# Identity products on TensorE ahead of the first rows of four stages

## The chip, the core and the metric

The kernel runs on one core of one Trainium2 chip. The metric is the device time of one launch in microseconds (us). Engines are named as in the profile: PE is TensorE, DVE is VectorE, ACT is ScalarE, POOL is GpSimd, SP is SyncE, and PEld is the loading of weights into PE.

## What is computed

Four residual layers over `x` of 64 sequences of 64 rows of 256 numbers, cut here to their lines:

```python
x = x + tanh(g_xattn[0]) * _L0_xattn_ref(layernorm(x), ctx, ...)   # 8 heads, rotary, softmax
x = x + tanh(g_ffn[0])   * _L0_ffn_ref(layernorm(x), ...)          # 8 experts, best 2 of each row
x = x + tanh(g_xattn[1]) * _L1_xattn_ref(layernorm(x), ctx, ...)   # linear attention, relu features
x = x + tanh(g_ffn[1])   * _L1_ffn_ref(layernorm(x), ...)          # causal attention, then 16 experts, best 4
```

The first layer takes its tokens in blocks of channels: keys and queries are projected, turned by rotary tables, multiplied into scores, put through a softmax and multiplied with the values. In an expert layer each row goes through the experts that a small product (the router) chooses for it.

## The kernel before

The program is a row of stages, one after another, each a block in which every engine has its own list of instructions and waits on semaphores: softmax attention (lines 412 to 905), the first experts with the linear attention behind them (954 to 1483), causal attention (1935 to 2568), and the second experts (954 again). At the end of a block all engines meet before the next one starts. There is no scheduler: PE does its work in the order in which the code is written, and a wait in that order holds up everything behind it.

**Softmax attention** goes over 32 tiles of 128 rows, which the code calls `n`, in a loop over `i` from -5 to 34, and each step of the loop does a different part of several tiles. For tile `n`, `project(n, False)` (L846, L847) and `project(n, True)` (L846, L847 again) multiply the normalised rows and the context with the weights, in full fp32, at step `i = n - 4`; DVE multiplies the two results with the cosine and sine tables (L721), POOL adds them (L600), and DMAs lay the sum out into `soft_rep` (L504). Then `both(i, k)`, eight times in a step, makes score products: L816 (`soft_pa`) for a later tile, whose maxima DVE takes (L735), and L809 (`soft_pb`) for tile `i`, for ACT's exponential (L630). `values` (L830) multiplies with the values and L881 projects them. While `i` is negative there is no tile `i`: `both` then makes no `soft_pb`, and before the second half of `i = -2` it makes nothing at all. PE begins the loop when `soft_shift` (DVE, L710) is there.

**Each expert stage** starts with `b = -2` and `b = -1`. `turn_rows` (L1427) turns the 128 rows of a block, which a DMA brings as `moe_xs`, `up` (L1440) multiplies them with an expert's two input matrices, and `down` (L1459) with its output matrix.

**Causal attention** starts with constants; PE waits for `ca_hn`, turns the rows (L2549), and then `project` (L2396) makes the queries and keys of 128 columns at a time, five to a unit: `p` counts them. Each result is copied by ACT to `ca_q_f` (L2174), which has two buffers; SP's DMAs swap its halves (L2082), and DVE and POOL put the rotation together.

The matrix that all of these stages hold for turning rows is the identity in fp32: `soft_ident_f`, `ident` of the experts (a slice of `moe_held`), and `ca_ident`.

Of the kernel before, what the change touches and what calls it, by code (L numbers as in the profile page):

```python
# [20 lines left out]
PART = 128  # L21
# [24 lines left out]
def hold(eng, sem, count, held):  # L46

    if not (isinstance(count, int) and count <= 0):
        eng.wait_ge(sem, count)
        if not isinstance(count, int):  # L50
            eng.sem_inc(held, 1)

LOWEST, MARK = -3.0e38, -3.2e38
# [357 lines left out]
def stage_softmax_attention(nc, x_in, x_out, ctx, c):  # L412
# [8 lines left out]
    HEADS, GROUPS, KC, T, HALF, PAIRS = 16, 4, 8, 256, 2, 8  # L421
# [6 lines left out]
    with st:  # L428
# [77 lines left out]
        with nc.Block() as block:  # L506
# [278 lines left out]
            def _(pe):  # L785
# [5 lines left out]
                def both(i, k):  # L791

                    n, m = (i + 1, k + 4) if k < 4 else (i + 2, k - 4)
                    if live(i) and k == 0:
                        pe.wait_ge(peak_in[i % 2], 64 * (i // 2 + 1))
                    if live(n) and m == 0:
                        pe.wait_ge(rep_in[n % 4], REP * (n // 4 + 1))
                    for h in range(2):
                        if live(i):  # L800
                            past(pe, prob_ready, 2 * (PAIRS * i + k) + h - 1)
                        if live(n):
                            past(pe, a_done, 2 * (PAIRS * n + m) + h - 1)
                        for c in range(HALF):
                            out = slice((2 * h + c) * T, (2 * h + c + 1) * T)
                            if live(i):
                                g, rows = pair(k)
                                of, at = slice(32 * rows[h], 32 * rows[h] + SPLIT + 1), T + c * PART
                                mm = pe.matmul(p_b[:, out], rep[of, i % 4, g, at:at + PART], rep[of, i % 4, g, 0:T],  # L809
                                               start=True, stop=True)  # L810
                                if c == HALF - 1:
                                    mm.then_inc(b_ready, 1)
                            if live(n):
                                g, rows = pair(m ^ 1)
                                of, at = slice(32 * rows[h], 32 * rows[h] + SPLIT), c * PART
                                mm = pe.matmul(p_a[:, out], rep[of, n % 4, g, at:at + PART], rep[of, n % 4, g, T:2 * T],  # L816
                                               start=True, stop=True)
                                if c == HALF - 1:
                                    mm.then_inc(a_ready, 1)
# [15 lines left out]
                def project(n, rotated):  # L835
                    if not live(n):
                        return
                    r = int(rotated)
                    if rotated:
                        pe.wait_ge(cos_done, 2 * (n + 1))  # L840
                    else:
                        pe.wait_ge(xn_ready, n + 1)
                        pe.wait_ge(c_in_s[n // LOAD % 4], 16 * (n // RING + 1))
                        past(pe, sin_done, 2 * n)
                        past(pe, y_ready, n - 6)
                    pe.matmul(p_x[1][:, 0:T], w_in[:, r, :], xn[:, n % 2, :], start=True, stop=True)  # L846
                    pe.matmul(p_x[1][:, T:2 * T], w_in[:, 2 + r, :], ct[:, n % RING, :], start=True, stop=True  # L847
                              ).then_inc(qkrot_ready if rotated else qk_ready, 1)

                for i in every:  # L850
                    both(i, 0)
                    project(i + 4, False)
                    both(i, 1)
                    values(i - 1, 3)
# [99 lines left out]
def experts(nc, name, x_in, x_out, w_gate, w_up, w_down, c, EXPERTS, HIDDEN, TOP, norm, skip=None, then=None):  # L954
# [36 lines left out]
    with st:  # L991
# [75 lines left out]
        with nc.Block() as block:  # L1067
# [322 lines left out]
            def _(pe):  # L1390
# [72 lines left out]

                owner = {}
                for b in range(-2, ALL + 1):
                    if b + 2 < ALL:
                        turn_rows(b + 2)
                    if 0 <= b + 1 < ALL:
                        n = b + 1
                        if n == START[1]:  # L1470
                            pe.wait_ge(route.expert_ready, 1)
                        owner[n % 3] = pe.value_load(expert_of[0:1, n:n + 1],
                                                     min_val=0, max_val=EXPERTS - 1)
                        up(n, owner[n % 3])
                    if 0 <= b < ALL:
                        turn_act(b)
                    if b >= 1:
                        down(b - 1, owner[(b - 1) % 3])
                    routing(b)
# [455 lines left out]
def stage_causal_attention(nc, x_in, z_out, c):  # L1935
# [19 lines left out]
    with st:  # L1955
# [102 lines left out]
        with nc.Block() as block:  # L2058
# [330 lines left out]
            def _(pe):  # L2389
                pe.wait_ge(const_in, 16 * NCONST)  # L2390
                pe.wait_ge(const_r, 2)

                def products(out, pairs, start=True, stop=True):
                    todo = [xy for lh, ll, rh, rl in pairs for xy in ((lh, rh), (lh, rl), (ll, rh))]
# [4 lines left out]
                def project(u, m):  # L2399
# [5 lines left out]
                        pe.wait_ge(wlo_ready, ALL_Q)  # L2405
                    if m == 0 and kp == 0:
                        pe.wait_ge(htlo_ready, 2 * (ch + 1))
                    past(pe, qf_ready, p - 1 if p < EARLY else p)
                    if m == 0 and kp == 1:
                        past(pe, route.ht_ready, 2 * min(ch - 1, ROUTED))  # L2410
# [234 lines left out]
```

## Time and profile before

| what | value |
|---|---|
| median of 3 runs | 2581.12 us (2579.25 to 2589.17) |
| the profiled execution's own time | 2571.76 us |
| its span, first to last instruction | 2569.9 us |
| PE busy | 2199.1 us, 86% of the span |
| DVE busy | 1835.5 us, 71% |
| ACT, POOL busy | 1154.2 us, 1104.7 us |
| mean granted clock of TensorE | 0.926 |

The profile is of one execution. A row of the timeline shows a start, a duration, the engine, the line, what it writes and reads, how many instructions the row joins, and in brackets how long the engine stood idle ahead of it and for whom.
### The profile page before, as it was taken

How to read it: one execution, taken by the hardware profiler on the slowest of the kernel's cores; microseconds unless marked ns; L12 is line 12 of the kernel's file. 1: busy time of each engine (PE TensorE's matmuls, PEld its weight loads, DVE VectorE, ACT ScalarE, POOL GpSimd, SP SyncE). 2: the span in 40 equal slices, each digit the busy share in tenths (PEclk: the TensorE clock that was granted, in tenths of full speed). 3: DMA queues.
4: the chain of work that ended last, by engine and by line, in shares of the span. 5: the costliest groups of instructions: out<-in, count | busy, mean ns of one | idle time of the engine just before them, and what ended most of it. 6: DMA issues, size and time to landing. Idle time of an engine off the chain costs nothing. (4 is left out here: it accounts for less than half of the span.)

```text
span 2569.9 us, 60412 instructions
## 1 busy us (share of the span) xinstructions
PE 2199.1 (86%) x20880; PEld 1669.5 (65%) x20880; DVE 1835.5 (71%) x3965; ACT 1154.2 (45%) x2509; POOL 1104.7 (43%) x1111
## 2 busy tenths in 40 slices
PE   6889888886878799993899998999988699999990
PEld 4555555543766577762677777777766577888880
DVE  4888988872557787765878878878787374545754
ACT  2677767664534233323444444444333264333330
POOL 3454555565154500002555445455487600334736
PEclk9888989975899899997999999999999799999995
DMA  5455554442469523212332332322334382445854
GB/s 115 108 134 139 149 142 133 118 137 76 126 198 296 150 88 103 77 38 53 82 88 56 83 84 62 84 73 69 79 99 115 123 266 83 139 142 183 265 170 147
DMA packets 250435, 313.10 MB, mean 122 GB/s; under 512 B 45216, under 2 KB 202912, under 8 KB 250144
## 3 DMA queue, kind: packets, MB, share of 16 engines
q1 hardware_dynamic: 189168, 219.11, 30.7%
q0 software_dynamic: 26624, 58.79, 8.2%
q10 hardware_dynamic: 34352, 31.34, 3.6%
q8 instruction: 180, 2.95, 0.5%
q14 instruction: 111, 0.91, 0.1%
HBM read 122.40 MB, written 102.24 MB: 87 GB/s over the span
## 5 line engine op out<-in xcount | busy, mean ns | idle before, releaser
L2126 POOL TENSOR_TENSOR ca_qk<-ca_qk,ca_q_swap 128x512 f32<-128x512 f32 x160 | 248.9, 1556 | 366.6 <-DVE ca_q_swap L2304 366.1
L735 DVE TENSOR_REDUCE soft_top<-soft_pa 128x2 fp32r<-128x512 f32 x512 | 327.9, 683 | 83.0 <-PE soft_pa L816 80.2
L630 ACT ACTIVATE soft_prob<-soft_pb 128x512 f32<-128x512 f32 x512 | 286.1, 594 | 171.3 <-PE soft_pb L809 169.5
L809 PE MATMUL soft_pb<-soft_rep 32*128 32x256 f32 x1024 | 207.3, 359 | 53.2 <-DVE soft_top L735 27.6
L809 PEld LDWEIGHTS soft_pb<-soft_rep 32*128 32x128 f32 x1024 | 135.4, 211 | 170.3 <-issue 73.5
L816 PE MATMUL soft_pa<-soft_rep 31*128 31x256 f32 x1024 | 217.1, 366 | 5.9 <-DVE soft_top L735 3.5
L1459 PE MATMUL moe_py<-moe_w_d,moe_at 128*128 x788 | 212.7, 385 | 1.4 <-issue 0.8
L1440 PE MATMUL moe_pgu<-moe_w_hi,moe_xt_hi 128*128 x472 | 192.8, 408 | 22.7 <-DVE moe_xt_lo L1357 13.0
L2396 PE MATMUL ca_py<-ca_w_hi,ca_ot_hi 128*128 128x256 f32 x512 | 156.7, 306 | 38.3 <-DVE ca_ot_lo L2325 38.0
L1363 DVE TENSOR_TENSOR moe_act_f<-moe_silu,moe_pgu 128x256 f32<-128x256 f32 (+1 forms) x236 | 88.6, 375 | 131.5 <-ACT moe_silu L1258 131.2
L2304 DVE TENSOR_TENSOR ca_q_swap<-ca_q_swap,ca_sin_q 128x512 f32<-128x512 f32 x128 | 117.2, 916 | 82.0 <-DMA ca_q_swap<-ca_q_f 81.7
L1258 ACT ACTIVATE moe_silu<-moe_pgu 128x256 f32<-128x256 f32 (+1 forms) x236 | 82.4, 349 | 200.0 <-PE moe_pgu L1440 198.2
L1440 PE MATMUL moe_pgu<-moe_w_hi,moe_xt_lo 128*128 x472 | 171.1, 362 | 0.0
L1440 PE MATMUL moe_pgu<-moe_w_lo,moe_xt_hi 128*128 x472 | 170.7, 362 | 0.0
L830 PE MATMUL soft_po<-soft_prob,soft_vaug 128*32 128x256 f32 x2048 | 163.8, 446 | 0.0
L2188 ACT ACTIVATE ca_ot_hi<-ca_po 128x512 fp32r<-128x512 f32 x128 | 69.6, 595 | 209.7 <-PE ca_po L2494 209.7
L2396 PE MATMUL ca_pp<-ca_ht_hi,ca_w_hi 128*128 128x512 f32 x312 | 138.1, 443 | 22.8 <-ACT ca_q_f L2174 19.4
L1179 POOL DMA_INDIRECT moe_yg<-moe_ys_rows,moe_held x112 | 115.0, 1027 | 86.7 <-DVE moe_ys L1370 37.5
L1357 DVE TENSOR_TENSOR moe_xt_lo<-moe_pt,moe_xt_hi 128x256 fp32r<-128x256 f32 x236 | 99.5, 422 | 71.5 <-ACT moe_xt_hi L1253 70.2
L2396 PE MATMUL ca_py<-ca_w_lo,ca_ot_hi 128*128 128x256 f32 x512 | 150.3, 294 | 0.0
L2396 PE MATMUL ca_py<-ca_w_hi,ca_ot_lo 128*128 128x256 f32 x512 | 150.2, 293 | 0.0
L364 POOL DMA_INDIRECT moe_rows<-moe_x_new,moe_held x80 | 78.1, 976 | 163.3 <-DVE moe_ys L1370 91.5
(377 smaller groups left out, 6252.7 us busy)
## 6 DMA issues: line engine op xcount, KB each, us to landing
ca_q_swap<-ca_q_f SPq DMA_DIRECT2D x640, 64.0 KB
moe_xs<-moe_rows SPq DMA_DIRECT2D x236, 128.0 KB
soft_rep<-soft_parts SPq DMA_DIRECT2D x378, 64.0 KB
moe_rows<-soft_blank SPq DMA_DIRECT2D x27, 768.0 KB
moe_ys_rows<-moe_ys ACTq DMA_DIRECT2D x134, 128.0 KB, 1.7
moe_ys<-moe_ys ACTq DMA_DIRECT2D x102, 128.0 KB, 2.6
moe_xd<-scratch SPq DMA_DIRECT2D x64, 128.0 KB, 2.7
ca_vs<-ca_v SPq DMA_DIRECT2D x32, 256.0 KB, 3.8
```

The costliest lines, as they stand in the source:

```text
L630: act.activation(prob[:, k % 4, h, :], p_b[:, 2 * T * h:2 * T * (h + 1)], ACT.Exp).then_inc(prob_ready, 1)
L735: dve.tensor_reduce(heads[:, j, :, g], p_a[:, 2 * T * h:2 * T * (h + 1)].rearrange("p (c s) -> p c s", c=HALF), AX, ALU.max).then_inc(a_do ...
L809: mm = pe.matmul(p_b[:, out], rep[of, i % 4, g, at:at + PART], rep[of, i % 4, g, 0:T], start=True, stop=True)
L816: mm = pe.matmul(p_a[:, out], rep[of, n % 4, g, at:at + PART], rep[of, n % 4, g, T:2 * T], start=True, stop=True)
L830: mm = pe.matmul(p_o[g % 2][32 * j:32 * j + 32, 0:T], vaug[:, i % 4, sc, 4 * g + j, :], prob[:, (2 * g + j // 2) % 4, j % 2, sc * T:(sc + ...
L1179: pool.indirect_dma_start(out=yg[:, t % HELD, k, :], out_offset=None, in_=ys_rows[h], in_offset=bass.IndirectOffsetOnAxis(ap=slot_id[:, t, ...
L1357: dve.tensor_tensor(xt_lo[:, b % 2, :, :], p_t[b % 2][:, 0:DIM].rearrange("p (k t) -> p k t", k=KC), xt_hi[:, b % 2, :, :].bitcast(fp32), ...
L1440: mm = pe.matmul(p_gu[b % 2][:, 0:W2], x[:, b % 2, k, :], w, start=(n == 0), stop=(n == 3 * KC - 1))
L1459: mm = pe.matmul(p_y[b % 2][:, 0:DIM], at[:, b % 2, m, :], w_d[:, bass.ds(e, 1), m, :].rearrange("p a d -> p (a d)"), start=(m == 0), stop ...
L2126: pool.tensor_tensor(qk[:, u % 2, m, :], qk[:, u % 2, m, :], q_swap[:, p % 2, :], ALU.add).then_inc(qk_ready, 1)
L2304: dve.tensor_tensor(out.rearrange("p (b s) -> p b s", s=SEQ), src.rearrange("p (b s) -> p b s", s=SEQ), tab[int(m == RQ)][:].unsqueeze(1). ...
L2396: mm = pe.matmul(out, x, y, start=start and n == 0, stop=stop and n == len(todo) - 1)
```

## The change

A helper `warm` multiplies a 128x128 fp32 identity by itself a number of times, into a PSUM region that nobody reads before it is written again. PE's list gets it in five places; nothing else changes.

```diff
+def warm(pe, out, of, times):
+
+    for _ in range(times):
+        pe.matmul(out, of, of, start=True, stop=True)
...
@@ softmax attention, in both(i, k), for each h and c
                                 if c == HALF - 1:
                                     mm.then_inc(b_ready, 1)
+                            elif i < 0:
+                                warm(pe, p_o[0][:, T:T + PART], ident_f[:], 1)
...
                 for i in every:
                     both(i, 0)
+                    if i < -1:
+                        warm(pe, p_o[0][:, T:T + PART], ident_f[:], 8)
                     project(i + 4, False)
...
@@ both expert stages
                 for b in range(-2, ALL + 1):
+                    if b < 0:
+                        warm(pe, p_y[1][:, 0:PART], ident, 6 if b == -2 else 4)
                     if b + 2 < ALL:
                         turn_rows(b + 2)
...
@@ causal attention
                 pe.wait_ge(const_r, 2)
+                warm(pe, p_s[:, 0:PART], ident[:], 28)
...
                         pe.wait_ge(htlo_ready, 2 * (ch + 1))
+                    if 0 < p < M5 + 3:
+                        warm(pe, p_s[:, 0:PART], ident[:], 2)
                     past(pe, qf_ready, p - 1 if p < EARLY else p)
```

That is 192 products in softmax attention (32 in the eight calls of `both` of each of five steps, and 8 in each of four steps), 10 in each expert stage, and 42 in causal attention (28, and 2 ahead of each of seven projections).

PE's list at the start of softmax attention before; L846 and L847 are the projections, L881 the values' projection, L816 the first score products:

```order
2 L846 MATMUL soft_px<-soft_xn,soft_w_in 128x256
3 L847 MATMUL soft_px<-soft_ct,soft_w_in 128x256
4 L846 MATMUL soft_px<-soft_xn,soft_w_in 128x256
5 L847 MATMUL soft_px<-soft_ct,soft_w_in 128x256
6 L846 MATMUL soft_px<-soft_xn,soft_w_in 128x256
7 L847 MATMUL soft_px<-soft_ct,soft_w_in 128x256
8 L846 MATMUL soft_px<-soft_xn,soft_w_in 128x256
9 L847 MATMUL soft_px<-soft_ct,soft_w_in 128x256
10 L881 MATMUL soft_px<-soft_w_in,soft_ct 128x128 x2
```

The same stretch now, where L58 is the added product and all other lines have moved down (L855, L856 and L892 are the projections):

```order
2 L58 MATMUL soft_po<-soft_ident_f 128x128 x52
3 L855 MATMUL soft_px<-soft_xn,soft_w_in 128x256
4 L856 MATMUL soft_px<-soft_ct,soft_w_in 128x256
5 L58 MATMUL soft_po<-soft_ident_f 128x128 x8
6 L855 MATMUL soft_px<-soft_xn,soft_w_in 128x256
7 L856 MATMUL soft_px<-soft_ct,soft_w_in 128x256
8 L58 MATMUL soft_po<-soft_ident_f 128x128 x32
9 L855 MATMUL soft_px<-soft_xn,soft_w_in 128x256
10 L856 MATMUL soft_px<-soft_ct,soft_w_in 128x256
11 L58 MATMUL soft_po<-soft_ident_f 128x128 x8
12 L855 MATMUL soft_px<-soft_xn,soft_w_in 128x256
13 L856 MATMUL soft_px<-soft_ct,soft_w_in 128x256
```

Ahead of the first projection there now stand 52 products, ahead of the second 8, ahead of the third 32. A little later each score product of the steps -2 and -1 has one in front of it, the first four here (L825 is the score product, L816 before):

```order
22 L58 MATMUL soft_po<-soft_ident_f 128x128 x5
23 L825 MATMUL soft_pa<-soft_rep 128x256
24 L58 MATMUL soft_po<-soft_ident_f 128x128
25 L825 MATMUL soft_pa<-soft_rep 128x256
26 L58 MATMUL soft_po<-soft_ident_f 128x128
27 L825 MATMUL soft_pa<-soft_rep 128x256
28 L58 MATMUL soft_po<-soft_ident_f 128x128
29 L825 MATMUL soft_pa<-soft_rep 128x256
```

Before, these score products stood next to each other. At the start of causal attention PE now has this list, in which L2565 are the transposes (L2549 before) and L2410 the projections (L2396 before):

```order
4741 L58 MATMUL ca_ps<-ca_ident 128x128 x28
4742 L2565 MATMUL ca_p_t<-ca_ident,ca_hn 128x128 x4
4743 L2565 MATMUL ca_pp<-ca_ident,ca_hn 128x128 x4
4744 L2410 MATMUL ca_pp<-ca_ht_hi,ca_w_hi 128x512
4745 L2410 MATMUL ca_pp<-ca_ht_lo,ca_w_hi 128x512
4746 L2410 MATMUL ca_pp<-ca_ht_hi,ca_w_lo 128x512
4747 L2410 MATMUL ca_pp<-ca_ht_hi,ca_w_hi 128x512
4748 L2410 MATMUL ca_pp<-ca_ht_lo,ca_w_hi 128x512
4749 L2410 MATMUL ca_pp<-ca_ht_hi,ca_w_lo 128x512
4750 L58 MATMUL ca_ps<-ca_ident 128x128 x2
```

Before, the list of this block began with the transposes, and the second projection followed the first directly.

## Rows read from the trace of the kernel before

**Rows 1.** Stretches: us, busy time per engine (instructions), PEclk, DMA share, GB/s.

```profile
0.00:71.00 71.00, 45.64 (x165) 30.22 (x166) 34.48 (x78) 20.23 (x29) 21.19 (x28) 1.00 0.53 115
8.00:58.76 50.76, 33.70 (x94) 22.54 (x95) 25.71 (x60) 12.83 (x17) 12.85 (x13) 1.00 0.44 77
1163.00:1183.00 20.00, 0.00 (x0) 0.00 (x0) 12.94 (x34) 9.93 (x14) 4.62 (x7) 0.50 0.18 47
2064.00:2100.00 36.00, 35.89 (x185) 29.26 (x184) 31.99 (x65) 29.26 (x67) 0.00 (x0) 1.00 0.98 324
```

**Rows 2.** Timeline of PE, first rows of softmax: start, us, what, [idle before].

```profile
10.80 1.19 PE L846 MATMUL soft_px<-soft_xn,soft_w_in 128*128 128x256 f32 x2 [3.26 <-ACT soft_xn L655]
13.82 1.22 PE L846 MATMUL soft_px<-soft_xn,soft_w_in 128*128 128x256 f32 x2 [0.97 <-DVE soft_by_cos L721]
...
34.59 0.80 PE L816 MATMUL soft_pa<-soft_rep 31*128 31x256 f32 x4 [2.45 <-DMA soft_rep<-soft_parts]
...
38.04 1.39 PE L816 MATMUL soft_pa<-soft_rep 31*128 31x256 f32 x4 [0.49 <-DVE soft_top L735]
39.62 1.39 PE L816 MATMUL soft_pa<-soft_rep 31*128 31x256 f32 x4 [0.18 <-DVE soft_top L735]
...
58.76 0.55 PE L809 MATMUL soft_pb<-soft_rep 32*128 32x256 f32 x1 [0.28 <-DVE soft_top L735]
```

**Rows 3.** Timeline of DVE, the same stretch.

```profile
7.66 0.28 DVE L710 TENSOR_SCALAR soft_shift<-soft_px,soft_cols,soft_gate 128x1 f32<-128x1 f32 x1 [0.50 <-PE soft_px L787]
...
38.87 1.29 DVE L735 TENSOR_REDUCE soft_top<-soft_pa 128x2 fp32r<-128x512 f32 x2 [0.28 <-PE soft_pa L816]
```

**Rows 4.** Timeline of PEld and PE: fp32 passes of 128 columns or fewer.

```profile
35.31 0.93 PEld L881 LDWEIGHTS soft_px<-soft_w_in,soft_ct 128*128 128x128 f32 x4 [0.23 <-issue]
70.64 0.53 PEld L881 LDWEIGHTS soft_px<-soft_w_in,soft_ct 128*128 128x128 f32 x4
70.70 0.66 PE L881 MATMUL soft_px<-soft_w_in,soft_ct 128*128 128x128 f32 x4
458.68 3.43 PEld L252 LDWEIGHTS soft_px<-soft_r_picked,soft_r_ones 128*128 128x128 f32 x30
```

**Rows 5.** Timeline of PE: fp32 passes of 256 columns in the second experts.

```profile
2251.57 1.03 PE L1459 MATMUL moe_py<-moe_w_d,moe_at 128*128 x4
```

**Rows 6.** Timeline of PE: one product in each tile of softmax.

```profile
52.37 0.69 PE L877 MATMUL soft_px<-soft_ident,soft_top 128*128 128x128 f32 x2
70.36 0.50 PE L877 MATMUL soft_px<-soft_ident,soft_top 128*128 128x128 f32 x2
...
104.47 0.44 PE L877 MATMUL soft_px<-soft_ident,soft_top 128*128 128x128 f32 x2
119.75 0.44 PE L877 MATMUL soft_px<-soft_ident,soft_top 128*128 128x128 f32 x2
```

**Rows 7.** Timeline around the start of causal attention, PE and DVE.

```profile
1157.81 1.13 PE L1818 MATMUL la_py<-la_w_out,la_o_t 128*128 128x256 f32 x4 [0.47 <-ACT la_o_t L1715]
1170.03 0.19 DVE L2249 CAST ca_mask_r<-ca_mask 128x64 fp32r<-128x64 f32 x1
1183.53 1.09 PE L2549 MATMUL ca_p_t<-ca_ident,ca_hn 128*128 128x128 f32 x4 [24.59 <-ACT ca_hn L2203]
...
1186.98 0.76 PE L2396 MATMUL ca_pp<-ca_ht_hi,ca_w_hi 128*128 128x512 f32 x1 [1.50 <-DVE ca_ht_lo L2385]
...
1190.10 0.40 PE L2396 MATMUL ca_p_t<-ca_ht_lo,ca_w_hi 128*128 128x512 f32 x1
```

**Rows 8.** Timeline of PE, starts of the two expert stages.

```profile
644.90 0.69 PE L1427 MATMUL moe_pt<-moe_held,moe_xs 128*128 128x128 f32 x2 [8.97 <-DMA moe_xs<-moe_rows]
...
2056.22 0.69 PE L1427 MATMUL moe_pt<-moe_held,moe_xs 128*128 128x128 f32 x2 [14.95 <-DMA moe_xs<-moe_rows]
...
2058.16 0.79 PE L1440 MATMUL moe_pgu<-moe_w_hi,moe_xt_hi 128*128 x1 [0.17 <-issue]
...
2063.87 0.40 PE L1448 MATMUL moe_pat<-moe_held,moe_act_f 128*128 128x128 f32 x2
```

## The prediction

> **What bounds the kernel now.** I read the shares of the engines first: PE is the busiest, but at the places that the change touches it is idle for part of the time, so each place has to be read for itself. Then the stretches and the timeline of PE there.
>
> *First rows of softmax.* From 8 us, when DVE's `soft_shift` ends (7.66 + 0.28) [rows 3], to 58.76, when the first `soft_pb` is made [rows 2], PE is busy 33.7 of 50.8 us [rows 1]. Its waits are short ones, for the normalised rows, for the cosine product and for `soft_rep` [rows 2]: a chain that goes from engine to engine and back. The column of the granted clock shows 1.00 up to 71 us [rows 1], but nothing is recorded so early, and the passes say otherwise: four loads of one shape take 0.93 us at 35.31 and 0.53 us at 70.64 [rows 4]. So until about 70 us PE runs at its lower level, 1.2 GHz, and the idle 17 us would grow to about 34 if its 33.7 us of work ran at the other.
>
> *Later stages.* Causal attention starts with PE idle for 24.59 us; the clock stands at 0.50 through 1163 to 1183 [rows 1, 7], and passes shorten at 1190.1 [rows 7]. The first experts' PE waits 8.97 us for its first rows, the second experts' 14.95; in the latter passes shorten at 2063.87 [rows 8].
>
> **The price of one added product.** It is two passes of 128 columns in fp32. Thirty loads of passes of that kind take 3.43 us, 0.114 each [rows 4], so 0.23 us a product at 2.4 GHz. The bound above is a short group: two products take 0.66 us from first start to last end, 0.33 each [rows 4]. The bound below is 0.21: the thirty loads less the tail of the last one. At 1.2 GHz four loads take 0.93 us [rows 4]; less the tail of the last that is about 0.21 a pass, 0.43 a product. I take 0.23, since PE will have long rows of them, as in the thirty, and 0.43 while the clock is still low. How long that is: in causal attention 3.1 us pass from the first projection at 1186.98 to the short pass at 1190.10 [rows 7], in the second experts 5.7 us from 2058.16 to 2063.87 [rows 8]. I take 5.
>
> The Trainium skill ("TensorE: Matmul & The Clock Gate", Part 4) says that transposes against an identity do not raise the clock in the way that other products do. Here the added ones are ordinary products, and no run here shows what a row of identity products alone does; by that rule, if it held for them, the rival "the clock stays down" below would be the result.
>
> **Softmax, step by step** (PE's list; 192 products):
>
> 1. Ahead of the first projection stand 52 products, and PE can start them at 8.0. 5 us at the low clock pass some 11.6 of them, the other 40.4 take 9.3: the first projection starts at 22.3. It started at 10.80 [rows 2]. So 11.5 us late; PE had only 3.26 us to give away there.
> 2. From there to the first score product PE has six projections, 92 products (8, 32, 8, 32, 8 and 4) and the values' projection. A projection is four passes of 256 columns: 1.03 us [rows 5], and about 1.0 when the next one follows. 6.0 + 92 x 0.23 + 0.5 = 27.7, so the first score product would start at 50.0, before at 34.59 [rows 2]: 15.4 late. Does another chain end later? From the second projection at 13.82 to the score product were 20.8 us [rows 2], through DVE, POOL, ACT and the DMAs into `soft_rep`; the second projection now starts at 22.3 + 1.0 + 1.8 = 25.1, so `soft_rep` is there at about 45. PE is last.
> 3. From there to `soft_pb`: before, 24.2 us, twelve pairs of score products. A pair takes 1.58 us (38.04 to 39.62): 0.83 until DVE starts on it (38.87), 0.65 for DVE's half of 1.29, and 0.1 back [rows 2, 3]. With the products in it PE needs 4 x (0.23 + 0.12) = 1.4 a pair (four score passes take 0.80 at the low clock [rows 2], so about 0.12 each at the high one), and DVE can start about as late as before, since four passes have come in front and its own run twice as fast. I take 1.6, so 19.2; the other work in the stretch was 24.2 - 19.0 = 5.2 and becomes about 2.9. Together 22.1: `soft_pb` starts at 72.1, before at 58.76: **13.3 us late**.
> 4. Then the row itself gains: with the clock up from the start. From one `L877` to the next, the first tile took 17.99 us, the next two 34.11 together, and the one after 15.28 [rows 6]. I take 16.5 for the first: **1.5 less**, between none and 2.7.
>
> Nothing takes the delay back later: all 32 tiles follow one after another, and all stages after them.
>
> **Causal attention.** The 28 products may start once `ca_mask_r` is there, 1170.2 [rows 7]: 5 us low and 16.4 x 0.23 = 3.8, so they end near 1179, hidden in the idle time before 1183.53; at 0.43 each they would end at 1182.2, still hidden. What they buy: the transposes and the first projection, 6.6 us from 1183.53 to 1190.10 with 1.50 of waiting among it [rows 7], are PE's at the low clock for at most 4.6 us on the path, of which half could go. But then PE stands idle again for 4.5 us, and the last time it stood idle, from 1158.94, the clock was down by 1163 [rows 1, 7]. So it may be down again before the transposes. **0.7 less**, between 2.3 less and 1 more: the two products ahead of each later projection cost at most 0.46 to 0.86 us each where PE does not wait, and there the swaps by SP's DMAs are later anyway.
>
> **Experts.** Six products at the low clock are 2.6 us, against idle times of 8.97 and 14.95 us [rows 8], a part of which lies before the block opens, so up to 0.6 may stick out; the four ahead of the second transposes are 1.7 us, hidden in the first stage, and in the second they push the first `up` back by about 0.6. What they buy is an earlier rise: in the second stage at most half of the 5.7 us from 2058.16 to 2063.87, 2.9. But from 2064 to 2100 the DMA engines are at 0.98 [rows 1], so PE will meet the next rows' transfers instead. **0.7 less** in the first (2 less to 0.6 more), **0.5 less** in the second (2.4 less to 0.6 more).
>
> **The sum**: 13.3 - 1.5 - 0.7 - 0.7 - 0.5 = 9.9 us more. Against the profiled execution's own 2571.76 that is 2581.7; the median of the runs is 9.4 above that execution, and I put the same 9.9 on it: **2591.0 us**, 0.4% slower. Low end: 5 us of low clock less 0.9, 0.21 for a product 2.6 less, pairs by 0.1 less 1.2, and the four gains at their best, 5.9 more of them: about 0 in all, 2581. High end, with 0.26 a product and the gains at their worst: 9.9 + 0.3 + 4 + 1 + 4.7, some 20, 2601.
>
> **Rivals.**
>
> - *Each product costs what a lone one does*, 0.33. Then 132 products ahead of the score products cost 13 more, and a pair becomes PE's, 4 x (0.33 + 0.12) = 1.8, 2.4 more over twelve: 2606. For it: only loads and short groups are seen, no row of fp32 products of 128 columns. Against: the thirty [rows 4]. 15%.
> - *The clock stays down.* 52 x 0.43 puts the first projection at 30.4; the way to the score products is 12 + 92 x 0.43 + 1 = 53, a pair 4 x 0.63 = 2.5, so 30 + 6.8 more: `soft_pb` at 120, 61 late, and nothing won elsewhere: 2643. For it: no row has identities alone. Against: ordinary products lift the clock at 1190 and 2064 [rows 7, 8]. 4%.
> - *The rows stay up: faster.* The clock, once raised early, might stay up through many tiles. A tile at the high level took 15.28, its neighbours 17.06 [rows 6], 1.8 apart. To win back 13.3 and end below by the 13 us that can be told, less the 3.4 of the other gains, takes 23 us, thirteen of 32 tiles. Twenty tiles would give 2581 + 13.3 - 36 - 2 = 2556. Against: nothing in a later tile is changed, and the two tiles after the first rise at 70 took 17.06 each. 5%.
> - *The products hide.* If PE's idle time took them all, no loss at the front: 2577. It speaks against it that 192 x 0.23 = 44 us do not go into 34. 8%.
>
> **Chances.** The forecast with its bounds has 68%. What a measurement can tell of this kernel is about 0.5%, 13 us: slower means above 2594. Of the forecast's cases a quarter lies there (a product of 0.25 or more, or the gains near their worst), 0.17, so slower is 0.17 + 0.15 + 0.04 = 0.36; faster 0.05; same the rest, 0.59. The range from 2577 to 2604 leaves out the clock's rival, the many rows, and most of the lone products: about 2 in 10.
>
> **What would show it.** The first `L855` (the projection) at about 22 instead of 10.8, the first score product near 50, the first `soft_pb` near 72, and shortened passes from 11 to 14 us on; in tile 1 and later the same times as before. In causal attention the transposes at 1183.5 plus the front's delay, with the clock either up or just fallen. The forecast is wrong if the first projection comes before 20 or after 27, if a pair takes 1.8, or if the tiles after the first change by more than noise.

## The result, and the profile after

| what | before | after |
|---|---|---|
| median of 4 runs of each, in turn | 2582.18 us (2579.25 to 2589.17) | 2626.52 us (2624.39 to 2632.64) |
| ratio | | 1.0183, interval 1.0159 to 1.0208 |
| the profiled execution's own time | 2571.76 us | 2627.59 us |
| mean granted clock | 0.926 | 0.918 |

The changed kernel is slower by 44 us, where 10 were forecast. All lines of the code have moved down: L58 is the added product, L855 and L856 are the projections (L846, L847 before), L825 is the score product `soft_pa` (L816), L816 is `soft_pb` (L809), and L888 is the product that each tile has once (L877). In the experiments they shift by a few lines more; the operands tell them apart.

The first rows of softmax on PE, timeline of the kernel after (start, us, what it is, idle time before). It answers to [rows 2]:

```profile
8.99 14.23 PE L58 MATMUL soft_po<-soft_ident_f 128*128 128x128 f32 x104 [0.54 <-DVE soft_shift L717]
23.05 0.60 PE L855 MATMUL soft_px<-soft_xn,soft_w_in 128*128 128x256 f32 x2
...
23.92 1.95 PE L58 MATMUL soft_po<-soft_ident_f 128*128 128x128 f32 x16
...
26.57 7.31 PE L58 MATMUL soft_po<-soft_ident_f 128*128 128x128 f32 x64
...
48.34 1.28 PE L58 MATMUL soft_po<-soft_ident_f 128*128 128x128 f32 x10
49.54 0.38 PE L825 MATMUL soft_pa<-soft_rep 31*128 31x256 f32 x1
49.85 0.49 PE L58 MATMUL soft_po<-soft_ident_f 128*128 128x128 f32 x2
50.27 0.38 PE L825 MATMUL soft_pa<-soft_rep 31*128 31x256 f32 x1
...
58.31 0.79 PE L58 MATMUL soft_po<-soft_ident_f 128*128 128x128 f32 x2
59.03 0.58 PE L825 MATMUL soft_pa<-soft_rep 31*128 31x256 f32 x1
59.54 0.80 PE L58 MATMUL soft_po<-soft_ident_f 128*128 128x128 f32 x2
60.26 0.58 PE L825 MATMUL soft_pa<-soft_rep 31*128 31x256 f32 x1
60.77 0.80 PE L58 MATMUL soft_po<-soft_ident_f 128*128 128x128 f32 x2
```

Up to the first score product all is as forecast: 64 passes take 7.31 us, 0.114 each, the two passes of a projection's row take 0.60 where they took 1.19 [rows 2], and the score product comes at 49.54. Then one *place*, an added product (two passes on 128 rows) and a score product (one pass on 31 rows), takes 0.73 us (49.54 to 50.27), and from 58.3 on 1.23 us (59.03 to 60.26). The forecast had 0.35. There are 48 places before the first `soft_pb`, which comes at 106.89 instead of 72.1.

The weight loads in the same stretch, kernel after, show what a place is made of:

```profile
60.26 0.28 PEld L825 LDWEIGHTS soft_pa<-soft_rep 31*128 31x128 f32 x1 [0.23 <-issue]
60.77 0.50 PEld L58 LDWEIGHTS soft_po<-soft_ident_f 128*128 128x128 f32 x2 [0.22 <-issue]
61.49 0.28 PEld L825 LDWEIGHTS soft_pa<-soft_rep 31*128 31x128 f32 x1 [0.22 <-issue]
```

Each load starts at the very time at which its product starts (60.26, 60.77), never ahead of it beside the product before, and the loader stands idle for 0.22 us at each change between 128 rows and 31, waiting for nothing that the trace shows. The same mark stood in the trace of before, in [rows 4], at the one load that followed score products ("35.31 ... [0.23 <-issue]"); the load of the same shape at 70.64 has none.

Stretches of the kernel after (us; busy time and instructions of PE, PEld, DVE, ACT and POOL; PEclk, DMA share, GB/s), against [rows 1]:

```profile
15.00:49.00 34.00, 34.00 (x284) 33.38 (x283) 6.32 (x20) 6.29 (x7) 6.12 (x6) 1.00 0.22 36
50.00:58.00 8.00, 8.00 (x36) 5.38 (x36) 3.53 (x6) 1.39 (x3) 2.08 (x2) 1.00 0.35 56
58.50:107.00 48.50, 48.50 (x124) 31.84 (x124) 14.69 (x26) 1.76 (x4) 3.08 (x3) 0.50 0.25 63
```

PE is never idle in any of the three, and yet the granted clock falls from 1.00 to 0.50 at 58.3, after 8.8 us of places, and stays there to the end of the stretch. This busy time holds the stops at the changes too: the score product of 49.54 is shown until 49.92, past the start of the next one at 49.85.

From the first `soft_pb` on no later tile has an added product; the delay is 49.2 us at tile 3, 40.4 at tile 12, 52.4 at tile 31, and 52 to 54 at the starts of the later stages. Two of these starts, timeline of PE after, against [rows 7] and [rows 8]:

```profile
1222.64 7.95 PE L58 MATMUL ca_ps<-ca_ident 128*128 128x128 f32 x56 [11.16 <-DVE ca_mask_r L2262]
1235.73 0.95 PE L2565 MATMUL ca_p_t<-ca_ident,ca_hn 128*128 128x128 f32 x4 [5.13 <-ACT ca_hn L2216]
...
1241.74 1.05 PE L58 MATMUL ca_ps<-ca_ident 128*128 128x128 f32 x4
1242.44 0.63 PE L2410 MATMUL ca_p_t<-ca_ht_hi,ca_w_hi 128*128 128x512 f32 x1
1242.91 0.40 PE L2410 MATMUL ca_p_t<-ca_ht_lo,ca_w_hi 128*128 128x512 f32 x1
```

```profile
695.37 2.90 PE L58 MATMUL moe_py<-moe_held 128*128 128x128 f32 x12 [7.01 <-PEq L2628]
698.06 0.64 PE L1438 MATMUL moe_pt<-moe_held,moe_xs 128*128 128x128 f32 x2
698.49 1.81 PE L58 MATMUL moe_py<-moe_held 128*128 128x128 f32 x8
700.81 0.44 PE L1438 MATMUL moe_pt<-moe_held,moe_xs 128*128 128x128 f32 x2 [0.51 <-DMA moe_xs<-moe_rows]
```

In causal attention the 28 products are hidden (PE waits 5.13 us more after them), but the short pass comes 7.2 us after the transposes, before 6.6 [rows 7]. In the first experts the first transposes come 53.2 us later than before, where tile 31 was 52.4 late, so the products ahead of them stick out by about 0.7; the second transposes wait for their DMA, and are 52.1 late.

### The profile page after: what moved, and what is told of

Read it like the earlier page. It is cut to its first block and busy times, and to the rows that moved or that the text cites. A ratio compares the mean times of both kernels' runs of the same rounds, so it can differ in the third digit from the quotient of the medians.

```text
span 2625.8 us, 61428 instructions
## 1 busy us (share of the span) xinstructions
PE 2278.0 (87%) x21388; PEld 1738.0 (66%) x21388; DVE 1840.2 (70%) x3965; ACT 1154.1 (44%) x2509; POOL 1108.6 (42%) x1111
## 5 line engine op out<-in xcount | busy, mean ns | idle before, releaser
L816 PE MATMUL soft_pb<-soft_rep 32*128 32x256 f32 x1024 | 208.5, 360 | 53.0 <-DVE soft_top L742 27.0
L816 PEld LDWEIGHTS soft_pb<-soft_rep 32*128 32x128 f32 x1024 | 136.6, 212 | 170.7 <-issue 71.7
L825 PE MATMUL soft_pa<-soft_rep 31*128 31x256 f32 x1024 | 229.1, 369 | 0.0
L1451 PE MATMUL moe_pgu<-moe_w_hi,moe_xt_hi 128*128 x472 | 192.1, 407 | 23.9 <-DVE moe_xt_lo L1368 13.3
L2410 PE MATMUL ca_py<-ca_w_hi,ca_ot_hi 128*128 128x256 f32 x512 | 153.0, 299 | 33.7 <-DVE ca_ot_lo L2338 33.3
L2410 PE MATMUL ca_pp<-ca_ht_hi,ca_w_hi 128*128 128x512 f32 x312 | 138.4, 443 | 25.9 <-ACT ca_q_f L2187 19.3
L825 PEld LDWEIGHTS soft_pa<-soft_rep 31*128 31x128 f32 x1024 | 142.5, 210 | 9.5 <-issue 8.1
L2187 ACT ACTIVATE ca_q_f<-ca_pp 128x512 f32<-128x512 f32 x156 | 92.8, 595 | 124.6 <-PE ca_pp L2410 115.0
```

Of the source, the lines that this page charges most:

```text
L1451: mm = pe.matmul(p_gu[b % 2][:, 0:W2], x[:, b % 2, k, :], w, start=(n == 0), stop=(n == 3 * KC - 1))
L2410: mm = pe.matmul(out, x, y, start=start and n == 0, stop=stop and n == len(todo) - 1)
```

## The experiments

The delay "at tile 3" below is that of the fourth tile's `L877` against 104.47 [rows 6], in the profiled execution: there the front is over and the later tiles have not yet drifted apart. (Tiles are counted from 0; the expectations call it the third.) Two kernels below whose softmax front takes the time that it took before are 0.2 and 0.0 late there. Softmax's 192 products are 144 ahead of the first score product and 48 beside score products.

**Which products cost.** Four kernels, each against the changed one. The first leaves out the 48 beside the score products:

```diff
-                            elif i < 0:
+                            elif i < 0 and not live(n):
```

> The changed kernel without the 48 products that stand between score products (32 in step -1, 16 in step -2); the 144 others of softmax, and those of the other stages, stay. Theory 'mix': the loss is made where 128-row fp32 products alternate with 31-row score products, since each alternation costs PE 0.2 us at the high clock and 0.3 at the low one, and since the clock falls there. Then the first score product is near 49 us as in the changed kernel, the stretch from there to the first soft_pb takes 22 to 25 us instead of 58, softmax is late by about 14 us at its third tile instead of 49, and the time is 2594 to 2598. Rival 'every product costs alike': three quarters of the products give three quarters of the delay, 37 us at the third tile, and about 2617.

Measured: tile 3 is 12.1 late; 2596.5 us, ratio 1.0039 (1.0009 to 1.0069). Two rows of its timeline of PE:

```profile
47.35 0.50 PE L825 MATMUL soft_pa<-soft_rep 31*128 31x256 f32 x4
...
56.10 0.80 PE L825 MATMUL soft_pa<-soft_rep 31*128 31x256 f32 x4
```

The same four passes take 0.50 us at first and 0.80 later, so the clock falls in this stretch even with nothing added in it. The second has only these 48, and nothing else of the change:

```diff
-                            elif i < 0:
+                            elif i < 0 and live(n):
```

> The kernel before with only the 48 products between score products. Theory 'mix': the first score product is where it was before, near 34.6 us; the stretch from there to the first soft_pb takes 57 to 62 us instead of 24.2, at the low clock throughout (48 places of 1.23 us), and softmax is late by 33 to 38 us at its third tile. Rival 'every product costs alike': a quarter of the 49 us, 12.

Measured: tile 3 is 41.1 late, 2629.1 us in one run. With no warmth from the products before, every place takes the long 1.23 us: 63.5 us from the first score product to `soft_pb`. Both lie above what was expected, by 1.5 and by 3 us. The third has the products of the experts and of causal attention alone:

> The changed kernel without any product in softmax: only the 10 in each expert stage and the 42 in causal attention. The prediction took 0.7, 0.7 and 0.5 us for their gains. The two traces side by side show a loss or gain below 1 us at the starts of the first experts and of causal attention, so 'nothing' expects a ratio of 0.999 to 1.001; the rival, that the other stages cost the 2 to 7 us by which the profile of the change is later at its end than at its causal attention, expects 1.001 to 1.003.

Measured: 2585.1 us, ratio 1.0013 (0.9987 to 1.0039); in its trace the first experts' first `up` comes 2.1 us sooner after tile 31 than before, and nothing of that can be told in the whole. Its softmax is the kernel's before, 0.2 late at tile 3; at tile 31 it is 8.5 late all the same. So a quarter of softmax's products makes three quarters to four fifths of the loss, and the 62 of the later stages do nothing that can be told.

**Why they cost: rows.** The 48 as products on 32 rows, the other operands the same in kind:

```diff
-                            elif i < 0:
+                            elif i < 0 and not live(n):
+                                warm(pe, p_o[0][:, T:T + PART], ident_f[:], 1)
                             elif i < 0:
-                                warm(pe, p_o[0][:, T:T + PART], ident_f[:], 1)
+                                q = 0
+                                pe.matmul(p_o[0][:, T:T + PART], ident_f[q:q + 32, :], ident_f[q:q + 32, :], start=True, stop=True)
```

> The changed kernel, in which the 48 products between score products use 32 rows of the identity (32x128 by 32x128, fp32, two passes as before) instead of 128. Theory 'row count': PE loses time when it changes between products of 128 and of 31 rows, so here nothing is lost by the change: a place takes 0.35 us at the high clock and 0.64 at the low one instead of 0.73 and 1.23, the stretch 22 to 36 us, softmax is late by 13 to 27 us at its third tile. Rival 'kind of data': it loses the time when it changes between fp32 and fp32r, so the places stay at 0.73 and 1.23 us and the delay at 45 us or more.

Measured: 30.6 us to `soft_pb`, tile 3 19.7 late. Its timeline of PE (L824 is the added product, L828 the score product):

```profile
47.41 0.37 PE L824 MATMUL soft_po<-soft_ident_f 32*128 32x128 f32 x1
47.41 0.38 PE L828 MATMUL soft_pa<-soft_rep 31*128 31x256 f32 x1
47.62 0.27 PE L824 MATMUL soft_po<-soft_ident_f 32*128 32x128 f32 x1
47.63 0.28 PE L828 MATMUL soft_pa<-soft_rep 31*128 31x256 f32 x1
```

Added product and score product now start together, 47.41 and 47.41. The added product lies on the first 32 rows, the score products by turns on four strips of 32 (`32 * rows[h]` in the kernel), so in most places the two can also run beside each other; where both lie on the first strip, a place at the high clock took 0.45 us (49.13 to 49.58), still less than 0.73. The granted clock fell here too: it is 0.50 from 53 to 78 us. With the data of another type, and one pass for two, but on 128 rows:

```diff
+                            elif i < 0 and not live(n):
+                                warm(pe, p_o[0][:, T:T + PART], ident_f[:], 1)
                             elif i < 0:
-                                warm(pe, p_o[0][:, T:T + PART], ident_f[:], 1)
+                                warm(pe, p_o[0][:, T:T + PART], ident[:], 1)
```

> As the changed kernel, but the 48 products beside the score products use the fp32r copy of the identity, on 128 rows and in one pass instead of two. Theory (each change between passes on 128 rows and passes on 31 rows stops PE, whatever the data): there are as many changes as before and one 128-row pass fewer at each place, so a place costs about 0.62 us at the high clock and 1.0 at the low one instead of 0.73 and 1.23; the stretch from the first score product to the first soft_pb takes about 46 to 50 us instead of 57.3, and tile 3 is 38 to 42 late; 33 us and 22 late if the clock should stay up. Rival (it is the fp32 data of the two passes that does not go with the score products): the stretch takes 25 to 28 us and tile 3 is 14 to 17 late.

Measured: places of 0.57 us at the high clock and 0.91 at the low one, 45.1 us to `soft_pb`, tile 3 32.7 late. Score products in its timeline of PE, two at either clock:

```profile
48.17 0.38 PE L827 MATMUL soft_pa<-soft_rep 31*128 31x256 f32 x1
...
48.74 0.38 PE L827 MATMUL soft_pa<-soft_rep 31*128 31x256 f32 x1
...
55.73 0.58 PE L827 MATMUL soft_pa<-soft_rep 31*128 31x256 f32 x1
...
56.65 0.58 PE L827 MATMUL soft_pa<-soft_rep 31*128 31x256 f32 x1
```

That is below what was expected of the changes (38 to 42 late), and far from the rival's 14 to 17. It is the number of rows that parts the two products, not the kind of data.

**The same work in another order.** Two products together ahead of each pair of score products, so half as many changes (a pair is here the two products of one half of `soft_pa`; the prediction's pair held two of these):

```diff
-                            elif i < 0:
+                            elif i < 0 and not live(n):
                                 warm(pe, p_o[0][:, T:T + PART], ident_f[:], 1)
+                            elif i < 0 and c == 0:
+                                warm(pe, p_o[0][:, T:T + PART], ident_f[:], 2)
```

> As the changed kernel, with the same 48 products, but two together ahead of each pair of score products instead of one ahead of each: half as many changes, the same passes. Theory (the changes cost): a pair with its two products takes about 1.07 us at the high clock and 1.87 at the low one instead of 1.46 and 2.47, the stretch is about 43 us instead of 57.3, and tile 3 is about 35 late. Rival (the added passes themselves cost, or DVE's round trip does): the stretch stays at 57 and tile 3 at 49 late.

Measured: 27.75 us to `soft_pb`, tile 3 17.9 late, 2597.3 us in one run. That is a pair for 1.07 us, as expected of the high clock, but from end to end: the clock did not fall, and the stretch is 15 us shorter than expected. Timeline and stretches of this kernel:

```profile
51.53 0.50 PE L827 MATMUL soft_pa<-soft_rep 31*128 31x256 f32 x2
51.96 0.71 PE L58 MATMUL soft_po<-soft_ident_f 128*128 128x128 f32 x4
52.60 0.50 PE L827 MATMUL soft_pa<-soft_rep 31*128 31x256 f32 x2
```

```profile
50.00:58.00 8.00, 8.00 (x48) 6.20 (x47) 4.99 (x9) 1.39 (x3) 1.26 (x1) 1.00 0.37 66
58.00:66.00 8.00, 8.00 (x45) 6.35 (x44) 5.62 (x12) 0.00 (x0) 0.55 (x1) 1.00 0.51 68
66.00:75.00 9.00, 9.00 (x55) 6.99 (x54) 5.82 (x11) 1.64 (x4) 2.54 (x2) 1.00 0.01 2
```

And all 48 in one row ahead of the first score product, and none beside score products:

```diff
+                        if n == 0:
+                            warm(pe, p_o[0][:, T:T + PART], ident_f[:], 48)
```

> As the changed kernel, with the same 192 products, but the 48 that stood beside the score products stand in one row ahead of the first of them: the same work, no changes among the score products. Theory (the changes cost): 48 products at 0.224 us are 10.8 us on top of the 12.1 that the kernel without these 48 was late, so the first score product starts at about 58, the first soft_pb at about 81, tile 3 is about 23 late, and the whole takes 2603 to 2609 us. Rival (so many products cost as much wherever they stand): 49 late and 2626.

Measured: first score product at 59.21, `soft_pb` at 81.92, tile 3 20.3 late, 2611.5 us, ratio 1.0102 (1.0058 to 1.0145). The front is as expected, 3 us better; the whole is 2.5 us above what was expected; in the profiled execution the delay grew by 13 between tile 3 and tile 31.

**More work, less time.** To part the price of a place from that of the clock, 24 products more than the changed kernel: two ahead of the first score product of a pair, one ahead of the second.

```diff
-                                warm(pe, p_o[0][:, T:T + PART], ident_f[:], 1)
+                                warm(pe, p_o[0][:, T:T + PART], ident_f[:], 2 if live(n) and c == 0 else 1)
```

> As the changed kernel, with 24 more products: ahead of the first score product of each pair two instead of one. Theory (of the 35 us that the stretch of score products took over the forecast, about half is the price of the changes at the high clock and half the fall of the clock, and two products together keep it up): a pair takes 0.224 us more than the 1.46 of the changed kernel at the high clock, 1.68, and the stretch 24 x 1.68 + 3.5 = 44 us instead of 57.3, so that more work makes it faster by some 13; tile 3 is about 36 late. Rival (the clock falls here too): a pair takes 2.9 us at the low clock, the stretch about 65, tile 3 57 late.

Measured: 42.2 us to `soft_pb` instead of 57.3, tile 3 30.5 late, 2607.9 us in one run. A pair takes 1.69 us (52.03 to 53.72), and the stretches stay at 1.00 throughout:

```profile
52.03 0.38 PE L825 MATMUL soft_pa<-soft_rep 31*128 31x256 f32 x1
...
52.76 0.38 PE L825 MATMUL soft_pa<-soft_rep 31*128 31x256 f32 x1
...
53.72 0.38 PE L825 MATMUL soft_pa<-soft_rep 31*128 31x256 f32 x1
```

```profile
58.00:66.00 8.00, 8.00 (x39) 5.79 (x39) 3.80 (x6) 0.00 (x0) 0.00 (x0) 1.00 0.53 74
66.00:75.00 9.00, 9.00 (x45) 6.40 (x43) 3.89 (x8) 0.00 (x0) 0.55 (x1) 1.00 0.00 1
75.00:85.00 10.00, 10.00 (x53) 7.26 (x52) 5.00 (x9) 1.65 (x4) 2.53 (x2) 1.00 0.01 3
```

**Is there anything to win?** Three kernels with softmax products alone, as many as PE's waits take. In the first, (6, 4, 7) ahead of the projections of normalised rows in the steps -5 to -3 and 2 ahead of the rotated ones; since step -5 projects nothing, 12 of them came to stand ahead of the first projection:

> Softmax alone, with 23 products that fit into the waits read from the trace of before: 6, 4 and 7 ahead of the first, second and third projection of normalised rows, 2 ahead of each rotated one among them, none beside score products, none in the other stages. Theory (the clock rises with identities, and products cost nothing where PE waits): the clock is up by about 15 us, the projections after that take 0.9 us for two instead of 2.0, the first score product comes at 31 to 34 us instead of 34.59, tile 3 is 1 to 4 us early, and the whole is the same or up to 0.15% faster, 2577 to 2583, less than can be told. Rival (the other engines' chains set the front, so there is nothing to win, and what sticks out is late): tile 3 is 0 to 3 us late.

Measured: 2582.4 us, ratio 0.9999 (0.9973 to 1.0026); tile 3 0.0 late. The clock rose, and nothing came of it. Its timeline of PE, and of ACT behind it:

```profile
12.78 0.60 PE L853 MATMUL soft_px<-soft_xn,soft_w_in 128*128 128x256 f32 x2
...
20.22 0.59 PE L854 MATMUL soft_px<-soft_ct,soft_w_in 128*128 128x256 f32 x2
20.65 0.61 PE L892 MATMUL soft_px<-soft_w_in,soft_ct 128*128 128x128 f32 x4
27.05 1.22 PE L853 MATMUL soft_px<-soft_xn,soft_w_in 128*128 128x256 f32 x2 [5.79 <-ACT soft_xn L662]
```

```profile
21.32 4.97 ACTq L511 DMA_DIRECT2D soft_rep<-soft_parts  x6
26.40 0.60 ACT L662 ACTIVATE soft_xn<-soft_xt,soft_low,soft_rstd 128x256 f32<-128x256 f32 x1 [6.46 <-issue]
```

PE has done two tiles' projections by 21.3 and then waits 5.79 us for `soft_xn`, which stands on ACT behind six DMA issues of 4.97 us together; in the kernel before the same projection started at 27.02. Where PE was made faster, ACT's list was last, and in that wait the clock fell again (1.22 at 27.05). So the second fills this wait too, starts with 6, and keeps two products beside each second pair of score products:

```diff
+                            if i < 0 and live(n) and h == 0 and c == 0:
+                                warm(pe, p_o[0][:, T:T + PART], ident_f[:], 2)
...
+                    if i < -1:
+                        warm(pe, p_o[0][:, T:T + PART], ident_f[:], (0, 6, 8, 24)[i + 5])
                     project(i + 4, False)
...
+                    if -5 < i < -1:
+                        warm(pe, p_o[0][:, T:T + PART], ident_f[:], 4)
                     project(i + 4, True)
+                    if i == -2:
+                        warm(pe, p_o[0][:, T:T + PART], ident_f[:], 8)
```

The products in the waits are 6 + 8 + 24 + 3 x 4 + 8 = 58; the 50 below was a slip.

> Softmax alone: 50 products in the waits of the first rows (6, 8 and 24 ahead of the first, second and third tile's projection, 4 ahead of each rotated one, 8 ahead of the first score product) and two ahead of every second pair of score products (24 more), none in the other stages. Theory (the clock stays up where PE has rows of 128-row passes often enough, and products that fit cost nothing): the first projection starts as in the kernel before, at about 10.8 us, the granted clock is 1.00 from 15 us to the first soft_pb, the first score product comes at 32 to 34.6 us, the stretch to soft_pb takes 20 to 23 us instead of 24.2, tile 3 is 2 to 5 us early, and the whole 2576 to 2581, up to 0.2% faster, at the edge of what can be told. Rival (the clock falls all the same, or other engines set the pace): tile 3 is 0 to 6 us late.

Measured: the first score product at 31.00, 3.6 early, but 29.3 us from there to `soft_pb`, where 20 to 23 were expected; tile 3 0.7 early; 2588.6 us, ratio 1.0049 (1.0025 to 1.0074). Its score products at the high clock, which goes down for the first time near 38.7:

```profile
32.92 0.51 PE L825 MATMUL soft_pa<-soft_rep 31*128 31x256 f32 x4
34.21 0.71 PE L58 MATMUL soft_po<-soft_ident_f 128*128 128x128 f32 x4 [0.77 <-DVE soft_top L742]
34.85 0.51 PE L825 MATMUL soft_pa<-soft_rep 31*128 31x256 f32 x4
```

Here the order of the list bites: two pairs of score products wait for DVE (0.77), and the added products stand behind that wait, not in it, so two pairs take 1.93 us (32.92 to 34.85) where before they took 1.58. The third leaves these out and keeps the 58:

> The 58 products of the run before that fit into the waits of the first rows (6, 8 and 24 ahead of the first, second and third tile's projection, 4 ahead of each of three rotated ones, 8 ahead of the first score product), and none beside score products. Theory (products that fit cost nothing, and a product beside score products is what cost): the first score product starts at about 31.0 as there; from it to soft_pb 23 to 24.2 us, since the clock falls some 5 us into it; soft_pb at 54 to 55, tile 3 is 3.5 to 5 us early, and the whole takes 2574 to 2582, 0.15% faster or the same. Rival (later tiles lose it again, by the clock's phase or by what other engines wait for): soft_pb is early as said, tile 31 is not, and the whole is 0 to 0.5% slower, as in the run before.

Measured: first score product at 33.12, 23.0 us to `soft_pb`, tile 3 2.7 us early, 2582.0 us, ratio 0.9996 (0.9973 to 1.0018). The list up to the first score product is that of the kernel before it, yet it came 2.1 us later than there: the first projection took 1.22 us at 11.45, in the other 0.90 at 10.86, so the clock rose later. So two expected times were missed, `soft_pb` (56.12, not 54 to 55) and tile 3 (3.5 to 5 early). This is the arrangement in which the front gains most, and 2.7 us of 2580 can't be told from none in the whole. No version beats the kernel before measurably.

## Why the prediction was wrong

**Step 1** (52 products ahead of the first projection, 22.3): right, 23.05; PE could begin the row at 8.99, 1 us later than the step took it, since all of this execution started that much later.

**Step 2** (first score product at 50.0, PE last): right, 49.54. The price of a product was right with it: 16 passes take 1.95 us and 64 take 7.31, so 0.22 each. The kernel without the 48 bears the two steps out: 12.8 late at the first score product, and 23.0 us from there to `soft_pb` instead of 24.2, so that 12.1 are left at tile 3.

**Step 3 failed**: `soft_pb` 48.1 us late instead of 13.3, all of it between 49.54 and 106.89. The step took four score passes in a row (0.80 at the low clock [rows 2]) and identity passes in a row, and added them: 0.23 + 0.12 a place. Passes of the two kinds do not follow each other like that. At the high clock a place takes 0.73, so each of its two changes costs (0.73 - 0.23 - 0.12) / 2 = 0.19 us; at the low clock (1.23 - 0.43 - 0.20) / 2 = 0.30. The pairs confirm it from the other side: half the changes save 2 x 0.73 - 1.07 = 0.39 for two. The rival "a lone product's price" came nearest in kind, but its 0.33 was put on all the products, and the 132 in rows never paid it.

**And the clock**, which step 3 took as raised for good, fell in the middle of it. How the 35 us over the forecast's 22.1 part: in the kernel with 24 products more, at 1.00 throughout, a pair takes 1.69 and the rest of the stretch 42.2 - 24 x 1.69 = 1.6. The changed kernel at that clock would take 24 x 1.46 + 1.6 = 36.6, an estimate from these rows; so about 15 us are the price of the changes and about 20 the fall of the clock. That the two are separate is shown by the runs, one trace each: 48 products in pairs keep the clock and 48 products one by one lose it. Losing it is no mark of the places, though: the kernel without the 48 lost it in this stretch as well (0.50 and 0.80 us for the same four passes), and still took 23.0 us from the first score product to `soft_pb`, with no added pass in it. So step 3 had no ground to take the clock as raised for good in this stretch. Why two orders keep it is not settled: PE is busy in them for the whole stretch, and so it is with the products one by one; whether the stops, which count as busy time, are the reason was not tested.

Was this to be seen before? The mark "[0.23 <-issue]" was in [rows 4], at a load that I used for its duration alone. The Trainium skill ("TensorEngine Tiling (Array Packing)", Key Properties) says that a change of the tiling mode, not only of the tile, drains TensorE; by its list of configurations 32 rows and 128 rows are different modes. The traces agree, with 0.19 and 0.30 us a change, for which the page has no figure. I had weighed another rule instead ("TensorE: Matmul & The Clock Gate", Part 4, on transposes against an identity); the products here are no transposes, and they raised the clock by themselves (0.60 us for the projection behind the first row), so the rival that hung on it fell.

**Step 4** (the first tile 1.5 less): nothing. From the first `soft_pb` to the second tile's `L877` the kernel before took 11.6 us (58.76 to 70.36) [rows 2, 6], the changed one 12.5 (106.89 to 119.35): the clock was low by then. In the kernel with pairs the clock fell right behind the first `soft_pb` (0.65 from 75 to 85 us), and it took 11.7 (76.69 to 88.41). In the kernel with 24 products more, where the clock was 1.00 up to 92 us, it took 10.6 (90.43 to 101.06). So about 1.0 of the 1.5 can be had where the clock stays up; here it did not.

**Causal attention and the experts** (1.9 less together). In causal attention the transposes are 52.2 late and the short pass 52.8, where the last product of linear attention was 52.6 late: 0.4 won, 0.3 lost. The forecast named the reason, PE idle again after the products and the clock down again, and it came so: 5.13 us of idle time, and first projections of 0.76 and 0.63 us as before. The first experts lost 0.7 at the first transposes and won 0.3 by the first `up`; their later first rows are set by their DMA. The second experts' block opened 53.3 late and their first `down` came 52.1 late, so 1.2 were won, but the fourth `down` was 53.1 late again.

**The sum** of 9.9 us is 44 by the medians. Of the 55.8 by which the two profiled executions differ, 49.2 stand at tile 3; the rest is later drift. That drift is open, but it is not the change's own: in several kernels the delay changes by 5 to 15 us between tile 10 and tile 31 in tiles whose code is the same, the kernel without any product in softmax goes from 0.2 late at tile 3 to 8.5 at tile 31, and executions of the kernel before differ by as much among themselves (2567.85 to 2592.35 us beside the last experiment). The ratio of 1.0049 in one of the last kernels is larger than anything that its front shows, and stays unexplained.

## What to carry to other kernels

A product that only keeps the clock up is priced by its neighbours: in a row of its kind it cost 0.22 us, between products on fewer rows 0.6 to 1.0, because each change between 128 rows and 31 stopped PE for 0.2 to 0.3 us. Put such products in rows, ahead of a wait and not behind it, no more than the wait takes, and ask first which engine is last once PE is fast: here it was ACT, with six DMA issues, and the gain was 2.7 us at best, in the front of one trace. When two numbers from rows of like work are added for work that alternates, look for a row in which the two kinds meet.

## What was not expected of the hardware

- A change between passes on 128 rows and passes on 31 rows takes 0.19 us at 2.4 GHz and 0.30 at 1.2, and the weight load starts only with its product (60.26 and 60.26); with 32 and 31 rows the two products start together (47.41 and 47.41).
- The granted clock fell to 0.50 behind a stretch in which PE was busy 8.00 of 8.00 us, and stayed there for 48.50 busy us of 48.50, with one added product ahead of each score product; with two ahead of each pair it stayed at 1.00. So a busy PE in the profile is no warrant of the high clock. The Trainium skill ("TensorE: Matmul & The Clock Gate", Part 1, What's actually happening) ties the low level to idleness. By the profile's busy time the measurement differs from that; but this time holds the stops at the changes, and whether PE counts as idle in them is open.
- More work took less time: 72 added products in the stretch 42.2 us, 48 of them 57.3, in another order 27.75.
- Six DMA issues on ACT's list took 4.97 us, 0.83 each, and the activation behind them on ACT began 0.1 us after the last of them (26.40).
